# Routing three quarters of the tokens of a mixture-of-experts layer inside the attention loop

## The chip, the cores and the metric

The kernel runs on one core of a Trainium2 chip. The metric is the device time of one execution in microseconds (us), as a median of several runs. The core has five engines that run their own instruction streams: TensorE (PE in the profile, with its weight loads as PEld), VectorE (DVE), ScalarE (ACT), GpSimd (POOL) and SyncE (SP). In this kernel SP issues the plain DMAs and POOL issues the indirect ones (scatters whose row numbers come from a tensor). The engines wait for each other through semaphores.

## What is computed

Three layers follow each other: path signatures projected to 128 features, attention inside sequences of 64 steps with 8 heads, and a feed-forward layer that adds one shared expert and one of 8 routed experts per token:

```python
h = tok(x, W, b)                          # signature, depth 4, then a projection
h = h + attn(layernorm(h), ...)
xf = layernorm(h)                         # 4096 tokens with padding, 128 features
logits = xf @ gate_w.T                    # 8 experts
wts, idx = jax.lax.top_k(logits, 1)       # one expert each
wts = softmax(wts)                        # of one value: 1
hh = silu(xf @ w1[e].T) * (xf @ w3[e].T)  # e = idx of the token
y = hh @ w2[e].T
y = y + gelu(xf @ sw1.T) @ sw2.T          # the shared expert, for all tokens
h = h + y
```

## The kernel before, in words

The 4096 tokens (64 sequences of 64) are 32 tiles of 128 tokens (`TILES`). The work has three stages.

**The loop.** Iteration i of 32 does attention for tile i, the signature features of tile i + 3 and the projection of tile i + 2, and finishes tile i - 1: its second layer norm gives `x2n`, which ACT keeps in `x2[:, t, 0:128]` (L561) and PE transposes. The transposed tile is spilled by SP to `x2_columns` (L368), and PE's `router` makes its 8 logits, which DVE stores (`keep_logits`, L888). Each engine has its own function `iteration`; the middle iterations run in a hardware loop (`Fori(2, TILES - 3)`, `Fori(1, TILES - 3)` on POOL) and the last three are written out. On POOL an iteration is: level 3 of the signature, `root(0, ...)` (the square root of the first norm, L458), the rest of level 3, `root(1, ...)` for tile i - 1, and `add_channels(i + 2)` (L449 to L453), whose sum PE's `accumulate` waits for. SP's queue holds, per iteration, `by_head` (four copies of the value rows, L363, the second half waiting for the attention of the tile before) and `spill` (L368).

**The tail of the loop and the shared expert.** The 32 tiles are 8 groups of 4 (`GROUPS`). `up(g)` makes 12 wide matmuls from the group's columns, ACT applies the gelu, `down(g)` makes 16 matmuls (32 records), and DVE adds the result to `h` (`add_shared`, L1030), which SP then writes to `out` (L398). The first two groups are started within the last iterations. While this runs, the tokens are routed. DVE picks each token's expert as a one-hot matrix `oh` (5 operations on 256 columns, L1043 to L1047), PE multiplies it by a strictly triangular matrix and by ones (ranks within a tile and totals of a tile), DVE turns these into a row number `pos` for each token (L1051 to L1071): tokens of one expert are consecutive, and each expert begins at a multiple of 128. POOL then scatters the 32 tiles of `x2`, one indirect DMA each (L507), into the DRAM tensor `sorted_rows` of 39 x 128 rows; a row is 128 values and the token's number (`ROW` = 129, 516 bytes). 39 tiles (`SORTED`) suffice for any routing. All rows were filled before with zeros and an impossible token number, by three DMAs of 13 tiles each ahead of the loop (L347), from a buffer that lies in `x2`; ACT waits for these before iteration 0 (L635).

**The experts.** For each of the 39 sorted tiles SP loads 128 rows (L404, L409), PE transposes them and multiplies them by the weights of the expert whose number it reads from the table `exp_i`, and POOL adds the result to `out` by an indirect DMA (L515), which drops rows with an impossible number. PE begins this stage when all 8 groups are added (`added`), and SP loads the first rows when group 5 is added and all scatters have landed.

The order is written out by hand: each engine executes its stream in order, so an instruction that waits holds up all that stand behind it on its engine.

Of the kernel before, what the change touches and what calls it, by code (L numbers as in the profile page):

```python
# [39 lines left out]
P = 128  # L40
# [28 lines left out]
FILL = SORTED // 3  # L69
SMALL_STEPS, NORM_STEPS, ROUTE_STEPS = 21, 9, 21  # L70
# [13 lines left out]
def build(nc, x_next, x_prev, w_low, w_high, tok_b, wqkv, u_qkv, wout_t, u_columns, b_out,  # L84
          scalars, gate_t, w13_t, w2_t, sw1_t, sw2_t, square, mask_c, steps, out):
    with ExitStack() as ctx:
# [7 lines left out]
        sorted_rows = nc.dram_tensor("sorted_rows", [SORTED * P, ROW], F32, kind="Internal").ap()  # L94
# [32 lines left out]
        fill, t3, t4, v3 = parts(x2[:].rearrange("p t r -> p (t r)"), FILL * ROW, in_c, in_c, in_c)  # L127
        fill = fill.rearrange("p (t r) -> p t r", r=ROW)
# [14 lines left out]
        stepc = sb("stepc", [P, EXPERTS + TILES + SORTED])  # L143
        rev_expert = stepc[:, 0:EXPERTS]
        tile_edges = stepc[:, EXPERTS:EXPERTS + TILES]
        tile_index = stepc[:, EXPERTS + TILES:]
# [55 lines left out]
        def taker(*hosts):  # L202
# [3 lines left out]
            def take(*shape):  # L206
# [3 lines left out]
                for part in parts:  # L210
# [20 lines left out]
        oh = late(TILES, EXPERTS)  # L231
        pick = late(TILES, EXPERTS)
        best = sb("best", [P, 2, TILES])
        tot = late(EXPERTS, TILES)
        incl = late(EXPERTS, TILES)
        zeros = late(EXPERTS * TILES)
        rt = sb("rt", [P, 8, EXPERTS])
        off = late(EXPERTS, TILES)
        over = late(EXPERTS, TILES)
        pos_f = late(TILES)  # L240
        pos = sb("pos", [P, TILES], U32)
        upt = late(SORTED, EXPERTS)
        exp_f = late(SORTED)
        exp_i = sb("exp_i", [P, SORTED], I32)
# [11 lines left out]
                    for n in range(2))  # L256
# [46 lines left out]
                                                  sem("scattered"))  # L303
        xg_hi, xg_lo, gelu_done = sem("x_group_hi"), sem("x_group_lo"), sem("gelu_done")
# [17 lines left out]
        def _(sp):  # L322
# [50 lines left out]

            by_head(0)
            with sp.Fori(0, 2 * GROUP) as t:
# [5 lines left out]
            with sp.Fori(2 * GROUP, TILES - 2) as t:  # L381
                by_head(t + 1)
                spill(t)
# [8 lines left out]

            for g in range(GROUPS):
# [6 lines left out]
                if g == GROUPS - 3:  # L400

                    sp.wait_ge(scattered, 16 * TILES)
                    for j in range(2):
                        sp.dma_start(rows[:, j, :], sorted_rows[j * P:(j + 1) * P, :]).then_inc(rows_in[j], 16)  # L404
            with sp.Fori(2, SORTED - 2, 2) as j:
                for k in range(2):
                    sp.wait_ge(rT_psum, j + (k - 1))
                    sp.wait_ge(id_kept, j + (k - 1))
                    sp.dma_start(rows[:, k, :], sorted_rows[bass.ds((j + k) * P, P), :]).then_inc(rows_in[k], 16)  # L409
            sp.wait_ge(rT_psum, SORTED - 2)  # L410
            sp.wait_ge(id_kept, SORTED - 2)
            sp.dma_start(rows[:, 0, :], sorted_rows[(SORTED - 1) * P:SORTED * P, :]).then_inc(rows_in[0], 16)
# [3 lines left out]
        def _(pool):  # L416
# [4 lines left out]
            nc.gpsimd.memset(fill[:, :, 0:DIM], 0.0)  # L421
            nc.gpsimd.memset(fill[:, :, DIM:ROW].bitcast(I32), NO_TOKEN).then_inc(filled, 1)
# [37 lines left out]

            def iteration(i, f, u, acc, prev=True):
# [29 lines left out]
            add_channels(1)  # L491
            iteration(0, True, True, True, False)
            with pool.Fori(1, TILES - 3) as i:
                iteration(i, True, True, True)
            iteration(TILES - 3, False, True, True)
# [1069 lines left out]
```

## Time and profile before

| | |
|---|---|
| median of 3 runs | 719.44 us (716.79 to 720.65) |
| the profiled execution: its own time | 718.2 us |
| its span, first to last instruction | 716.2 us |
| mean granted TensorE clock | 0.971 |
| PE busy | 653.1 us, 91% |
| PE weight loads busy | 521.1 us, 73% |
| DVE busy | 414.3 us, 58% |
| ACT busy | 295.8 us, 41% |
| POOL busy | 321.6 us, 45% |
| DMA packets, volume | 40993, 44.79 MB |

The page gives each engine's busy time, the same in 40 equal slices of the span, the DMA queues, the chain of work that ended last, and the costliest groups of instructions with the idle time ahead of them and what ended it. Views of single stretches give the busy times between two points, and the timeline lists the instructions in order. "issue" as a releaser means that the engine waited for nothing that the profile shows. PE multiplies at 2.4 GHz when the granted clock is 1.0 and at 1.2 GHz when it is 0.5. An fp32 matmul is recorded as two.

### The profile page before, as it was taken

How to read it: one execution, taken by the hardware profiler on the slowest of the kernel's cores; microseconds unless marked ns; L12 is line 12 of the kernel's file. 1: busy time of each engine (PE TensorE's matmuls, PEld its weight loads, DVE VectorE, ACT ScalarE, POOL GpSimd, SP SyncE). 2: the span in 40 equal slices, each digit the busy share in tenths (PEclk: the TensorE clock that was granted, in tenths of full speed). 3: DMA queues.
4: the chain of work that ended last, by engine and by line, in shares of the span. 5: the costliest groups of instructions: out<-in, count | busy, mean ns of one | idle time of the engine just before them, and what ended most of it. 6: DMA issues, size and time to landing. Idle time of an engine off the chain costs nothing.

```text
span 716.2 us, 13835 instructions
## 1 busy us (share of the span) xinstructions
PE 653.1 (91%) x3960; PEld 521.1 (73%) x3993; DVE 414.3 (58%) x1087; ACT 295.8 (41%) x701; POOL 321.6 (45%) x336
## 2 busy tenths in 40 slices
PE   5989999999999999999999999988753989999993
PEld 4767878887888778878887888766741867777772
DVE  7876667666766666667666666663710234455451
ACT  4234453445344443544454445437520434334440
POOL 3454455444545454544454445320376005444553
PEclk9999999999999999999999999999975799999998
DMA  8951112212211121112111211122621112322230
GB/s 315 223 197 30 38 33 47 48 37 62 53 42 37 33 59 37 37 33 62 33 37 33 62 33 37 35 62 67 208 83 52 46 48 40 42 40 41 37 41 5
DMA packets 40993, 44.79 MB, mean 63 GB/s; under 512 B 6416, under 2 KB 29712, under 8 KB 40592
## 3 DMA queue, kind: packets, MB, share of 16 engines
q1 hardware_dynamic: 34336, 40.34, 21.5%
q0 software_dynamic: 6640, 4.22, 4.2%
q8 instruction: 10, 0.16, 0.1%
q14 instruction: 7, 0.06, 0.0%
HBM read 16.78 MB, written 11.44 MB: 39 GB/s over the span
## 4 chain that ended last, share of the span: by engine, by line
PE 84%; issue 6%; DVE 5%; POOL 2%; ACT 1%; DMA 0%; SPq 0%; POOLq 0%; DVEq 0%
PE bank L1136 75%; PE bank L1448 3%; PE bank L1192 2%; PE bank L1338 2%; POOL z L449 1%; PE bank L1431 1%; PE bank L1251 1%; PE bank L1242 0%; PE bank L1197 0%; PE bank L1196 0%; POOL z L451 0%; DVE ident_b L960 0%; DVE z L833 0%; POOL out L515 0%; DVE vow L728 0%
## 5 line engine op out<-in xcount | busy, mean ns | idle before, releaser
L1136 PE MATMUL bank<-whigh,uth 128*128 128x512 f32 x512 | 167.6, 408 | 1.4 <-DVE lowt L728 1.4
L1136 PEld LDWEIGHTS bank<-whigh,uth 128*128 128x128 f32 x512 | 91.5, 188 | 27.3 <-issue 7.7
L515 POOL DMA_INDIRECT out<-z,ids x39 | 60.8, 1559 | 94.4 <-ACT z L691 94.1
L1136 PE MATMUL bank<-whigh,utl 128*128 128x512 f32 x256 | 101.0, 395 | 0.0
L458 POOL TENSOR_TENSOR rstd<-rstd,powers 128x1 f32<-128x1 f32 x64 | 35.2, 550 | 141.2 <-DVE rstd L820 83.7
L449 POOL TENSOR_TENSOR z<-z 128x512 f32<-128x512 f32 x32 | 42.2, 1320 | 94.0 <-DVE z L833 94.0
L1136 PE MATMUL bank<-xT,qkw 128*128 128x128 f32 x512 | 62.4, 275 | 0.0
L1109 DVE COPY xvp<-bank 128x512 f32<-128x512 f32 x39 | 27.0, 692 | 59.5 <-PE bank L1448 59.5
L1136 PEld LDWEIGHTS bank<-xT,qkw 128*128 128x128 f32 x512 | 59.7, 192 | 0.1
L833 DVE TENSOR_TENSOR z<-bank,v 128x512 f32<-128x512 f32 x64 | 44.1, 690 | 22.7 <-PE bank L1136 18.3
L1136 PEld LDWEIGHTS bank<-whigh,utl 128*128 128x128 f32 x256 | 48.1, 188 | 11.6
L1136 PE MATMUL bank<-whigh,vow 128*128 x117 | 49.0, 527 | 0.0
L567 ACT ACTIVATE xqk<-bank,fac 128x512 f32<-128x512 f32 x64 | 43.9, 689 | 7.2 <-PE bank L1136 5.9
L585 ACT ACTIVATE prob<-prob 128x512 f32<-128x512 f32 x32 | 20.2, 633 | 62.1 <-DVE prob L909 62.1
L591 ACT COPY pt<-bank 128x512 f32<-128x512 f32 x32 | 18.8, 588 | 64.2 <-PE bank L1338 64.2
L842 DVE TENSOR_TENSOR h<-bank,tokb 128x128 f32<-128x128 f32 x32 | 9.3, 292 | 59.8 <-PE bank L1136 59.8
L1136 PE MATMUL bank<-vow,xTh 128*128 128x512 f32 x128 | 42.8, 416 | 1.1 <-ACT xqk L567 1.1
L680 ACT ACTIVATE z<-bank 128x512 f32<-128x512 f32 x39 | 23.3, 598 | 49.2 <-PE bank L1136 30.2
L444 POOL TENSOR_TENSOR e3l<-e,e3h 128x512 fp32r<-128x512 f32 x31 | 40.4, 1304 | 6.2 <-DVE xn L854 4.9
L1136 PEld LDWEIGHTS bank<-xvp,pt 128*64 128x64 f32 x512 | 30.1, 137 | 17.8 <-issue 17.4
L1136 PE MATMUL bank<-levels,xvp 128*128 x312 | 41.4, 276 | 0.7 <-ACT z L691 0.5
L574 ACT COPY xvo<-bank 128x512 f32<-128x512 f32 x64 | 37.7, 588 | 10.2 <-PE bank L1136 8.8
(204 smaller groups left out, 1437.4 us busy)
## 6 DMA issues: line engine op xcount, KB each, us to landing
xvp<-xvo SPq DMA_DIRECT2D x128, 128.0 KB, 2.3
w<-w_t SPq DMA_DIRECT2D x1, 4096.0 KB, 19.3
sorted_rows<-x SPq DMA_DIRECT2D x3, 838.5 KB, 18.0
prob<-sorted_rows SPq DMA_DIRECT2D x39, 64.5 KB
w<-w_high SPq DMA_DIRECT2D x4, 512.0 KB, 5.9
x_columns<-x2t SPq DMA_DIRECT2D x32, 64.0 KB, 1.6
xg_in<-x_columns SPq DMA_DIRECT2D x8, 256.0 KB
levels<-w_t SPq DMA_DIRECT2D x1, 2048.0 KB, 7.5
```

The costliest lines, as they stand in the source:

```text
L444: G.tensor_tensor(e3l[:], e3[:], e3h[:].bitcast(F32), ALU.subtract).then_inc(e3_lo, 1)
L449: G.tensor_tensor(z4[:], z[:, 0:4, :], z[:, 4:8, :], ALU.add).then_inc(tree, 1)
L458: G.tensor_tensor(rstd[:, n, 1:2], rstd[:, n, 0:1], powers[:, 0:1], ALU.pow) \
L515: nc.gpsimd.indirect_dma_start(out=out[:, :], out_offset=bass.IndirectOffsetOnAxis(ap=ids[:, j:j + 1], axis=0), in_=y[:, j % 2, :], in_off ...
L567: A.activation(xqk[:, :, 4 * n:4 * n + 4, :], B[5 + n][:].rearrange("p (s h k) -> p s h k", s=2, h=4), ACT.Copy, scale=fac[:, 1:2]).then_i ...
L574: A.copy(xvo[:, n, :, :].rearrange("p c d -> p (c d)"), B[7 - 2 * n][:]) \
L585: A.activation(prob[:], prob[:], ACT.Exp).then_inc(exp_done, 1)
L680: nc.scalar.activation(act[:, k, :], B[1 + 2 * k][:], ACT.Silu).then_inc(silu_done, 1)
L833: V.tensor_tensor(z[:, cs, :], B[1 + half][:].rearrange("p (c d) -> p c d", c=4), spread(v[:, bass.ds(s, 1), cs].rearrange("p o c -> p (o ...
L1109: V.tensor_copy(hidT[:, k, :, :].rearrange("p c t -> p (c t)"), B[5][:]).then_inc(hT_sb, 1)
L1136: return T.matmul(out_, lhsT, rhs, start=start, stop=stop)
L1448: last = T.transpose(B[5][:, col(c)], hid[:, k, col(c)], ident)
```

## The change

24 of the 32 tiles (`EARLY`) are routed and scattered while the loop still runs. The rows now go to a region of 4096 rows per expert, so that a tile's rows can be placed before the totals are known: `sorted_rows` grows from 39 to 264 slabs of 128 rows. A table `row_i`, filled on DVE, gives each of the 39 expert tiles the first of its rows, and SP reads it for each load.

- The three fills ahead of the loop become 24 fills of 11 slabs (726 KB each), one per iteration 0 to 23 on SP's queue behind the spill, from a buffer `blank` of one row per partition. ACT's wait for the fills goes; POOL waits for them before the first scatter.
- DVE does the choice of the expert for 24 tiles at the end of iteration 25, the running sums at the end of 26, the row numbers at the end of 27. PE does the two rank matmuls (192 columns) in iteration 26, ACT copies them out of the bank.
- POOL issues the 24 scatters in iterations 28 (3, at its end), 29 (3 after `root(0)`, 2 after `root(1)`, 3 after `add_channels`), 30 (3 after `root(0)`, 6 after `root(1)`) and 31 (4 after `root(1)`); the last 8 follow after the loop.
- The same steps for 8 tiles stay after the loop (64 columns in place of 256), with one more sum for the base; `count`, the tile table and the new row table follow behind the row numbers.
- The hardware loops are cut: PE and ACT have `Fori(2, 26)`, iteration 26 written out, `Fori(27, 29)`; DVE has 25 to 28 written out, POOL 28.

```diff
-FILL = SORTED // 3
+EARLY = 24
+FILL, FILLS = 11, 24
+SLABS = FILL * FILLS
+CHOOSE_AT, RANK_AT, PLACE_AT, SCATTER_AT = EARLY + 1, EARLY + 2, EARLY + 3, EARLY + 4
...
@@ sync
-            sp.wait_ge(filled, 1)
-            for n in range(SORTED // FILL):
-                sp.dma_start(sorted_rows[n * FILL * P:(n + 1) * FILL * P, :].rearrange("(t p) r -> p t r", p=P),
-                             fill).then_inc(fill_sent, 16)
...
+            def fill(t):
+                sp.dma_start(sorted_rows[bass.ds(t * (FILL * P), FILL * P), :].rearrange("(n p) r -> p n r", p=P),
+                             spread(blank[:], 1, [P, FILL, ROW])).then_inc(fill_sent, 16)
...
+            with sp.Fori(2 * GROUP, FILLS) as t:
+                by_head(t + 1)
+                spill(t)
+                fill(t)
...
+            def load_rows(j, k):
+                row = sp.value_load(row_i[0:1, bass.ds(j, 1)], min_val=0, max_val=(SLABS - 1) * P)
+                sp.dma_start(rows[:, k, :], sorted_rows[bass.ds(row, P), :]).then_inc(rows_in[k], 16)
...
@@ gpsimd
+            def scatter(tiles):
+                for t in tiles:
+                    nc.gpsimd.indirect_dma_start(
+                        out=sorted_rows[:, :], out_offset=bass.IndirectOffsetOnAxis(ap=pos[:, t:t + 1], axis=0),
+                        in_=x2[:, t, :], in_offset=None).then_inc(scattered, 16)
...
                 if f:
                     level3_rest(i + 3)
+                if is_tile(i, SCATTER_AT + 1):
+                    scatter(range(3, 6))
+                if is_tile(i, SCATTER_AT + 2):
+                    scatter(range(11, 14))
                 if prev:
                     root(1, ln2, i - 1)
+                if is_tile(i, SCATTER_AT + 1):
+                    scatter(range(6, 8))
+                if is_tile(i, SCATTER_AT + 2):
+                    scatter(range(14, 20))
+                if is_tile(i, SCATTER_AT + 3):
+                    scatter(range(20, EARLY))
                 if u:
                     add_channels(i + 2)
+                if is_tile(i, SCATTER_AT):
+                    pool.wait_ge(pos_ready, 1)
+                    pool.wait_ge(x2_kept, EARLY)
+                    pool.wait_ge(ids_written, 1)
+                    pool.wait_ge(fill_sent, 16 * FILLS)
+                    scatter(range(3))
+                if is_tile(i, SCATTER_AT + 1):
+                    scatter(range(8, 11))
...
@@ scalar
+                if is_tile(i, RANK_AT):
+                    a.wait_ge(rank_psum, 1)
+                    A.copy(ranks_early.rearrange("p n m -> p (n m)"), B[6][:, 0:2 * EARLY * EXPERTS]) \
+                        .then_inc(rank_kept, 1)
...
@@ vector
+            def running(ts, counts, tot_, incl_, part):
+                n = ts.stop - ts.start
+                start, count, base = (rt[:, 3 * part + m, :] for m in range(3))
+                rstep(V.tensor_copy(tot_, counts.rearrange("p t e -> p e t")))
+                rstep(V.tensor_tensor_scan(incl_.rearrange("p e t -> p (e t)"), tot_.rearrange("p e t -> p (e t)"),
+                                           zeros[:, 0:n * EXPERTS], 0.0, ALU.add, ALU.add))
+                V.memset(start[:, 0:1], 0.0)
+                rstep(V.tensor_copy(start[:, 1:EXPERTS], incl_[:, 0:EXPERTS - 1, n - 1]))
+                V.tensor_tensor(count, incl_[:, :, n - 1], start, ALU.subtract)
+                rstep(V.tensor_tensor(base, slab_start, start, ALU.subtract))
+                rstep(V.tensor_tensor(incl_, incl_, tot_, ALU.subtract))
+                if part:
+                    rstep(V.tensor_tensor(base, base, rt[:, 1, :], ALU.add))
+
+            def place(ts, ranks, oh_, pick_, tot_, incl_, pos_, part):
+                n = ts.stop - ts.start
+                rstep(V.tensor_tensor(incl_, incl_, spread(rt[:, 3 * part + 2, :], 2, [P, EXPERTS, n]), ALU.add))
+                rstep(V.tensor_tensor(pick_, incl_.rearrange("p e t -> p t e"), ranks, ALU.add))
+                rstep(V.tensor_tensor(pick_, pick_, oh_, ALU.mult))
+                rstep(V.reduce_sum(pos_, pick_, axis=AX))
+                V.tensor_copy(pos[:, ts], pos_).then_inc(pos_ready, 1)
...
+            choose(slice(EARLY, TILES), oh, pick)
+            d.wait_ge(rank_psum, 2)
+            running(slice(EARLY, TILES), te_bank[1], tot, incl, 1)
+            place(slice(EARLY, TILES), te_bank[0], oh, pick, tot, incl, pos_f, 1)
...
@@ tensor
+                if is_tile(i, RANK_AT):
+                    pe.wait_ge(route, CHOOSE_STEPS)
+                    n = EARLY * EXPERTS
+                    mm(B[6][:, 0:n], below, oh_early[:].rearrange("p t e -> p (t e)"))
+                    mm(B[6][:, n:2 * n], ones, oh_early[:].rearrange("p t e -> p (t e)")).then_inc(rank_psum, 1)
...
-            with pe.Fori(2, TILES - 3) as i:
+            with pe.Fori(2, RANK_AT) as i:
+                iteration(i, True, True, True)
+            iteration(RANK_AT, True, True, True)
+            with pe.Fori(RANK_AT + 1, TILES - 3) as i:
```

## Rows read from the trace of the kernel before

**Rows 1.** The page, part 2: 40 slices of 17.9 us; digits are tenths.
```profile
PE   5989999999999999999999999988753989999993
PEclk9999999999999999999999999999975799999998
```
**Rows 2.** Stretches: length, busy us (x instructions) of PE, PEld, DVE, ACT, POOL; clock, DMA.
```profile
512.30:524.20 11.90, 11.42 (x76) 10.33 (x77) 5.87 (x12) 4.12 (x8) 9.22 (x9) 1.00 0.46 133
524.20:556.50 32.30, 10.58 (x28) 6.05 (x26) 1.90 (x4) 3.93 (x7) 22.54 (x23) 0.56 0.21 65
```
**Rows 3.** Timeline inside the second stretch: start, length, engine, operation [idle before].
```profile
541.08 0.29 PEld L1136 LDWEIGHTS bank<-vow,sw 128*128 128x128 f32 x1 [1.12 <-issue]
541.77 0.59 PE L1136 MATMUL bank<-vow,sw 128*128 128x512 f32 x1 [0.82 <-issue]
```
**Rows 4.** The tile pos: the scatters; durations in ns, then first and last start in us.
```profile
L507 POOL DMA_INDIRECT sorted_rows<-x,pos x32: 954/959/1363, 512.3 to 552.6; - x32
```
**Rows 5.** DMA queues from 520 to 556: packets, MB, share of 16 engines.
```profile
q0 software_dynamic: 866, 1.79, 15.3%
q1 hardware_dynamic: 672, 0.52, 4.9%
```
**Rows 6.** Timeline of the shared-FFN groups, before and after the slow stretch.
```profile
512.78 3.07 PE L1136 MATMUL bank<-vow,sw 128*128 128x512 f32 x12 [3.02 <-DVE vow L728]
...
563.33 0.48 PE L1136 MATMUL bank<-uth,sw 128*128 128x512 f32 x1
...
569.71 3.05 PE L1136 MATMUL bank<-vow,sw 128*128 128x512 f32 x12
...
576.16 0.61 PE L1136 MATMUL bank<-sw,xqk 128*128 128x128 f32 x4
...
579.94 0.69 DVE L1030 TENSOR_TENSOR h<-h,bank 128x512 f32<-128x512 f32 x1 [2.88 <-PE bank L1136]
```
**Rows 7.** Timeline of the routing chain after the loop, on DVE and PE.
```profile
502.56 0.42 DVE L1044 TENSOR_TENSOR e<-logits,best 128x256 f32<-128x256 f32 x1
...
505.16 1.03 PE L1136 MATMUL bank<-levels,sq 128*128 128x256 f32 x4
...
506.75 0.69 DVE L1052 TENSOR_TENSOR_SCAN g<-e,g 128x256 f32<-128x256 f32 x1
...
507.68 0.17 DVE L1058 TENSOR_TENSOR rt<-g,rt 128x8 f32<-128x8 f32 x1
```
**Rows 8.** Timeline of DVE between two trips of the loop.
```profile
462.22 0.29 DVE L842 TENSOR_TENSOR h<-bank,tokb 128x128 f32<-128x128 f32 x1 [1.89 <-PE bank L1136]
```
**Rows 9.** Timeline of POOL, iterations 29 to 31.
```profile
471.65 1.27 POOL L449 TENSOR_TENSOR z<-z 128x512 f32<-128x512 f32 x1 [2.36 <-DVE z L833]
...
476.69 0.55 POOL L458 TENSOR_TENSOR rstd<-rstd,powers 128x1 f32<-128x1 f32 x1 [1.88 <-DVE rstd L850]
481.68 0.55 POOL L458 TENSOR_TENSOR rstd<-rstd,powers 128x1 f32<-128x1 f32 x1 [4.44 <-DVE rstd L820]
...
499.13 0.55 POOL L458 TENSOR_TENSOR rstd<-rstd,powers 128x1 f32<-128x1 f32 x1 [3.98 <-DVE rstd L820]
```
**Rows 10.** The fills: issue times (ns), landing; then SP's queue from 24 to 28.
```profile
L347 SPq DMA_DIRECT2D sorted_rows<-x x3: 433/4568/5203, 11.9 to 17.6; - x3
DMA to landing us min/median/max: 13.1/18.0/18.7
q1 hardware_dynamic: 1451, 0.74, 124.9%
```
**Rows 11.** Timeline of SP's queue in the loop.
```profile
80.25 2.39 SPq L363 DMA_DIRECT2D xvp<-xvo  x4
87.85 0.34 SPq L368 DMA_DIRECT2D x_columns<-x2t  x1
94.48 2.39 SPq L363 DMA_DIRECT2D xvp<-xvo  x4
```
**Rows 12.** Waits on SP's queue in the expert stage: us in total, times, longest.
```profile
SPq L408 <- DVE ids L1097: 83.8, 34, 4.4
```

More of the change, by code:

```diff
@@ L380, in _ @@
             load_group(1)
-            with sp.Fori(2 * GROUP, TILES - 2) as t:
+            with sp.Fori(2 * GROUP, FILLS) as t:
+                by_head(t + 1)
+                spill(t)
+                fill(t)
+            with sp.Fori(FILLS, TILES - 2) as t:
                 by_head(t + 1)
@@ L400, in _ @@
                 if g == GROUPS - 3:
+                    sp.wait_ge(pos_ready, 4)
                     sp.wait_ge(scattered, 16 * TILES)
                     for j in range(2):
[L404 removed]
+                        load_rows(j, j)
             with sp.Fori(2, SORTED - 2, 2) as j:
@@ L491, in _ @@
             add_channels(1)
+            nc.gpsimd.iota(x2[:, :, DIM:ROW].bitcast(I32), pattern=[[P, TILES], [1, 1]], base=0,
+                           channel_multiplier=1).then_inc(ids_written, 1)
             iteration(0, True, True, True, False)
-            with pool.Fori(1, TILES - 3) as i:
+            with pool.Fori(1, SCATTER_AT) as i:
                 iteration(i, True, True, True)
+            iteration(SCATTER_AT, True, True, True)
             iteration(TILES - 3, False, True, True)
@@ L498, in _ @@
             root(1, ln2, TILES - 1)
-            nc.gpsimd.iota(x2[:, :, DIM:ROW].bitcast(I32), pattern=[[P, TILES], [1, 1]], base=0,
-                           channel_multiplier=1).then_inc(ids_written, 1)
-            pool.wait_ge(pos_ready, 1)
+            pool.wait_ge(pos_ready, 2)
             pool.wait_ge(x2_kept, TILES)
-            pool.wait_ge(ids_written, 1)
-            for t in range(TILES):
-                nc.gpsimd.indirect_dma_start(
-                    out=sorted_rows[:, :], out_offset=bass.IndirectOffsetOnAxis(ap=pos[:, t:t + 1], axis=0),
-                    in_=x2[:, t, :], in_offset=None).then_inc(scattered, 16)
+            scatter(range(EARLY, TILES))
             for g in range(GROUPS):
@@ L639, in _ @@
             iteration(1, True, True, True, False)
-            with a.Fori(2, TILES - 3) as i:
+            with a.Fori(2, RANK_AT) as i:
+                iteration(i, True, True)
+            iteration(RANK_AT, True, True)
+            with a.Fori(RANK_AT + 1, TILES - 3) as i:
                 iteration(i, True, True)
@@ L892, in x_group_lo, with rstep, choose @@
                 remainder(xgl[k], xg_in[:, k, :], xgh[k], xg_lo)
+            n_route = 0
+            def rstep(ins):
+                nonlocal n_route
+                ins.then_inc(route, 1)
+                n_route += 1
+                d.wait_ge(route, n_route)
+            def choose(ts, oh_, pick_):
+                te = [P, ts.stop - ts.start, EXPERTS]
+                top, first = best[:, 0, ts], best[:, 1, ts]
+                rstep(V.tensor_reduce(top, logits[:, ts, :], AX, ALU.max))
+                rstep(V.tensor_tensor(pick_, logits[:, ts, :], spread(top, 2, te), ALU.is_equal))
+                rstep(V.tensor_tensor(pick_, pick_, spread(rev_expert, 1, te), ALU.mult))
+                rstep(V.tensor_reduce(first, pick_, AX, ALU.max))
+                rstep(V.tensor_tensor(oh_, spread(rev_expert, 1, te), spread(first, 2, te), ALU.is_equal))
+            def running(ts, counts, tot_, incl_, part):
[18 more added lines that the diff above has]
+                V.tensor_copy(pos[:, ts], pos_).then_inc(pos_ready, 1)
             def iteration(i, f, u, acc, prev=True, older=True):
@@ L935, in iteration @@
                     features_lo(i + 3)
+                te_early = ranks_early.rearrange("p n (t e) -> p n t e", e=EXPERTS)
+                if is_tile(i, CHOOSE_AT):
+                    d.wait_ge(lg_sb, EARLY)
+                    choose(slice(0, EARLY), oh_early[:], pick_early)
+                if is_tile(i, RANK_AT):
+                    d.wait_ge(rank_kept, 1)
+                    running(slice(0, EARLY), te_early[:, 1], tot_early, incl_early, 0)
+                if is_tile(i, PLACE_AT):
+                    place(slice(0, EARLY), te_early[:, 0], oh_early[:], pick_early, tot_early, incl_early,
+                          pos_early, 0)
             n_norm = 0
@@ L1012, in _ @@
             iteration(1, True, True, True, True, False)
-            with d.Fori(2, TILES - 3) as i:
+            with d.Fori(2, CHOOSE_AT) as i:
+                iteration(i, True, True, True)
+            for i in range(CHOOSE_AT, TILES - 3):
                 iteration(i, True, True, True)
```

114 lines of the change are left out of this document (51 added, 63 removed).

## The prediction, made before the changed kernel ran

> **What bounds the kernel now.** I read the slices first. PE is nearly full in all of them except for two places: the start, and the slices around three quarters of the span, where it falls to 3 tenths while its granted clock falls too [rows 1]. Cut into stretches, the second place has a sharp edge. From 512.3 to 524.2 PE is busy 11.4 of 11.9 us; in the next 32.3 us only 10.6, with 28 matmuls, and at a mean clock of 0.56, close to the lower level of 1.2 GHz [rows 2]. That is the shared expert, whose work is all available. The timeline says what kind of idleness it is: single weight loads and matmuls, 0.70 us apart, each released by "issue", so no semaphore of this kernel and no operand is being waited for [rows 3]. DVE, ACT and SP only wait for PE there. What else runs is POOL: the 32 scatters, from 512.3 to 552.6, of 0.96 us with some 0.3 us between them, as 31 starts take 40.3 us [rows 4]. The last ends at 553.6, and PE is back to speed some 4 us later. The DMA engines aren't full: the scatters' queue takes 15% of them, the other 5% [rows 5]. So what holds PE isn't bandwidth. Scatters side by side with slow PE issue is a coincidence in time, with one oddity: for the first 12 us of scattering PE wasn't slowed.
>
> **What the slow stretch costs.** After it, PE needs 6.38 us per pair of an up and a down (563.33 to 569.71), and the last down takes some 3.75 us (576.16 to 579.9) [rows 6]. From 512.78 there are 5 pairs and one down left: 5 x 6.38 + 3.75 = 35.65 us, which would end at 548.4. It ends at 579.9. The stretch costs 31.5 us, the slow clock included. The experts can't start earlier, since they wait for the last group; behind it they need what they need now (136 us of the span).
>
> **The routing chain after the loop.** DVE's operations on 256 columns take 0.42 us, the scan 0.69, those on 8 columns 0.17 [rows 7]; some 20 of them hold `x_group_lo(3)` back, and PE waits 3.0 us for it at 512.8 [rows 6]. PE's own rank matmuls take 1.03 us [rows 7]. With 64 columns PE's part falls to a quarter, 0.26 us (-0.77). DVE's chain behind the ranks, 11 short operations at about 0.2 us, is an estimate of 2.4 us from these rows; it then ends inside `down(1)` (3.7 us) and the 3.0 us wait goes. Gain together 3.8 us, if the loop costs nothing.
>
> **What the loop pays, by engine.** PE: 192 columns in iteration 26, 1.03 x 0.75 = 0.8 us, all on its path. ACT: one copy out of the bank between the exponential and `x_hi`; ACT idles there, free. DVE: 5 operations of 192 columns (0.35 us and a hop of 0.04: 2.0 us) at the end of iteration 25, 1.8 us in 26, 1.8 us in 27. The next thing DVE does is `keep_logits` and then a wait of 1.9 us for PE's `accumulate` [rows 8]; that wait is the cover. What sticks out is 0.1 us in each, 0.3 us in all; with no cover it would be 5.6 us.
>
> POOL: each scatter is taken at 1.26 us, the first 1.66 [rows 4]. I laid them into POOL's timeline [rows 9], where what counts is the instruction behind each burst. In iteration 28 three scatters end at 464.5, `root(0)` for tile 30 is late by 1.0 us, and DVE has slack for that. In 29: the first three and two delay `add_channels(31)` by 0.35 us (due at 471.65), which PE's `accumulate` passes on: +0.35. The three behind it run to 478.95, but `root(0)` of tile 31 is due at 476.69: 2.3 us late, of which DVE absorbs 1.1: +1.2 us through the softmax to PE's transposes. In 30 the three before `root(1)` (due at 481.68) add 0.4, since PE waits for x2n there; the six behind it end at 491.5 and meet no one before 494. In 31 the four delay the last `root(1)` (499.13) by 1.1. Together 3.0 us. Loop in all: 0.8 + 0.3 + 3.0 = 4.1, less rounding 3.8 to 4.1. That takes back the 3.8 us of the routing chain. The bounds of the scatter's duration are its rows' ends, 0.95 and 1.36 us [rows 4]; at the upper end the bursts are a third longer and cost 3 us more. A gain is excluded there, as nothing that follows a burst gets earlier.
>
> Here the Trainium skill speaks against the change. SBUF — State Buffer, section "Who interferes with whom", says that GpSimd, which writes the descriptors of its DMAs, is locked out while VectorE runs an operation in a two-port mode. Taken fully, 24 scatters that each wait for a DVE operation would be longer by that. The rows bear it out little: with DVE half busy most scatters still took 0.96 us. The sum goes by the rows.
>
> **The fills.** Three fills of 838 KB go from before the loop. Nothing waited for them: ACT's wait ended long before its first iteration. In their place are 24 of 726 KB. While fills had the queue alone it moved 0.74 MB in 4 us with all engines full [rows 10], so a fill occupies them for about 4 us. It goes out behind the spill (87.9 in the trip shown) and the next copies behind it are issued at 94.5 [rows 11], 6.6 us later: the fill has drained by then. If not, these copies land later; ACT's next overwrite of the buffer gives them some 4.6 us beyond their landing time. Issuing took 0.43 us with the ring free and up to 5.2 us with it full [rows 10]; both end within the 6.6 us. Cost taken: 0. Bounds: 0 to 1 us in each of 24 if they don't drain. SP's table read for each row load is unseen so far; PE's reads of such a table show as 0.24 us of "issue", and SP idles 2.5 us per tile in the expert stage [rows 12]. Free. The tables on DVE come behind the row numbers and have 35 us until they are read.
>
> **The last 8 scatters** run from about 511.5 for 10.2 us and land some 3 us later: before PE slowed in the old kernel (12 us in). I take them as free; by the old price of a slow stretch (31.5 us lost in 32.3) the worst is 10 us.
>
> **Sum.** Loop +3.8, routing chain -3.8, slow stretch -31.5: span 716.2 - 31.5 = 684.7, own time 718.2 - 31.5 = 686.7. The median is 1.2 us above the profiled time: 687.9. Own range of this case, from the bounds: 683 to 694. Forecast: 688.
>
> **Rivals.**
> (a) A part of the slow stretch stays. PE issue suffers under every burst that lasts, whether in iteration 30 (9 scatters almost in a row, some 11 us) or after the loop (8 scatters, 10 us). For: PE slowed only after 12 us, so length matters, and near-continuous scattering from 461 to 491 is longer than that. Against: the gaps of up to 3 us, in which POOL adds channels. Losing 7 to 26 of the 31.5 us: 695 to 714, middle 703.
> (b) The slow stretch moves into the loop as a whole. This is the one that ends slower. The place is iterations 28 to 31, where PE has four times the instructions per us left to issue. If PE slows from the first scatter on, 24 scatters (30.6 us) and 8 (10.2) lose 5/6 of their time: 34 us, and POOL's 3.8 us are no longer hidden; with the clock at its lower level behind each, 720 to 728, 725 in the middle. It decides at the point where the 12 us of grace don't renew in a gap. The old stretch of 32 us did 5 us of work; that is where the 5/6 come from [rows 2].
> (c) The slowness has nothing to do with scatters, but with where PE's instructions lie: it began in the middle of a written-out loop body, 12 us behind the start of the scatters. Then it stays or turns up elsewhere: 716 to 723. Against: it ended with the scatters, although the body was then only a quarter through, and the queues show no packet of an instruction queue in the stretch [rows 5]. The Trainium skill, Runtime: NRT & Kernel Launch, section "Instruction fetch mechanics", says that the engines' instructions are streamed in blocks and that a branch out of the loaded blocks stalls; no row here shows a fetch in flight while PE crawls.
> (d) The fills don't drain between spill and copies. If one took the 18 us that fills took from issue to landing at the start, behind the loads [rows 10], instead of 4, each trip of 14.2 us (80.25 to 94.48) would stretch to 18 [rows 11]: 24 x 4 = 96 us slower, some 810.
>
> **Chances.** Forecast 0.62, better than its range 0.02; (a) 0.19; (c) 0.05; (b) 0.09, of which 0.02 within the 0.5%; (d) 0.03. Within 0.5% (716 to 723, about what a measurement of this kernel can tell from no change): 0.07. Slower by more: 0.10. Faster by more: 0.83. Range: 683 to 714, which holds the forecast and (a), 0.81.
>
> **What would show it.** Right: between the last iteration and the experts PE has no row with 0.7 us steps of "issue", the shared-expert groups follow at 6.4 us, the clock stays 1.0; iterations 0 to 24 keep their 14.2 us; from the end of iteration 27 to the first `up` after the loop PE loses 3 us, at `root(0)` of tile 31. (a): single-file PE rows beside the bursts of 6 or 8. (b): the same in 29 to 31. (c): the same with no scatter near. (d): trips longer than 14.2 us with ACT's copy waiting for a DMA. It would be wrong if the slow issue needs only a scatter, not a row of them, or if the loop's POOL order costs more than the instruction behind each burst.

## The result and the profile after

| | before | after |
|---|---|---|
| median | 719.43 us (716.79 to 720.65, 4 runs) | 692.41 us (691.7 to 695.3, 4 runs) |
| profiled execution: own time, span | 718.2, 716.2 us | 691.94, 690.1 us |
| mean granted clock | 0.971 | 0.985 |
| PE busy | 653.1 us, 91% | 647.0 us, 94% |
| DMA packets, volume | 40993, 44.79 MB | 70133, 59.70 MB |

The ratio of the times is 0.964 (95% interval 0.962 to 0.966). The forecast was 688; the measured time is 4.4 us above that and inside the forecast's own range of 683 to 694.

The page of after, part 2, in slices of 17.3 us. The hole of [rows 1] is gone, in PE and in its clock:

```profile
PE   5999999999999999999999999999789989999993
PEclk9999999999999999999999999999999999999997
```

What is left in its place are two shallower slices, from 483 to 518 us. POOL's scatters, by the tile `pos` (durations in ns, first and last start in us), now lie mostly ahead of that place, where [rows 4] had all of them in one row from 512.3 to 552.6:

```profile
L485 POOL DMA_INDIRECT sorted_rows<-x,pos x32: 956/962/1303, 464.4 to 526.8; - x32
```

To see where the rest went I used SP's spill of each tile as a mark, since it appears once per iteration in both kernels. First after, then before:

```profile
399.80 0.34 SPq L372 DMA_DIRECT2D x_columns<-x2t  x1
...
461.27 0.34 SPq L372 DMA_DIRECT2D x_columns<-x2t  x1
...
507.98 0.34 SPq L372 DMA_DIRECT2D x_columns<-x2t  x1
```
```profile
400.84 0.34 SPq L368 DMA_DIRECT2D x_columns<-x2t  x1
...
457.75 0.34 SPq L368 DMA_DIRECT2D x_columns<-x2t  x1
...
500.85 0.34 SPq L368 DMA_DIRECT2D x_columns<-x2t  x1
```

At 400 us after is 1.0 us ahead, at the end of the loop 7.1 us behind. With the shared-expert groups behind it, the account is (in us; the measured parts are rounded one by one):

| part of the span | predicted | measured |
|---|---|---|
| start, to the spill at 72 us | 0 | -1.5 |
| iterations with a fill | 0 | +0.5 |
| iterations 25 to 28 (ranks, DVE's steps) | +1.1 | +4.6 |
| iterations 29 to 31 (POOL's bursts) | +3.0 | +3.6 |
| last spill to `up(3)` | -3.8 | -2.2 |
| `up(3)` to the last group | -31.5 | -31.1 |
| experts | 0 | +0.1 |
| span | -31.5 (its terms add up to -31.2) | -26.1 |

Two parts of the loop, one after another. PE in iteration 27: the scores wait 1.42 us for `keep_logits`, and DVE's timeline shows what stands ahead of that copy.

```profile
435.94 1.08 PE L1217 MATMUL bank<-xqk,xT 128*64 128x512 f32 x4 [1.42 <-DVE logits L938]
```
```profile
432.49 0.57 DVE L966 COPY tail<-tail 128x192 f32<-128x192 f32 x1
433.09 1.32 DVE L967 TENSOR_TENSOR_SCAN tail<-tail,zeros 128x192 f32<-128x192 f32 x1
...
434.93 0.36 DVE L973 TENSOR_TENSOR tail<-tail 128x192 f32<-128x192 f32 x1
435.32 0.17 DVE L938 COPY logits<-bank 128x8 f32<-128x8 f32 x1
```

The scan of 192 columns takes 1.32 us, where the one of 256 columns in [rows 7] took 0.69. POOL in iteration 30, part of its timeline (start, length, [idle before]):

```profile
481.73 0.96 POOL L485 DMA_INDIRECT sorted_rows<-x,pos  x1 [0.30 <-issue]
482.72 0.57 POOL L479 TENSOR_TENSOR rstd<-rstd,powers 128x1 f32<-128x1 f32 x1
483.48 1.10 POOL L485 DMA_INDIRECT sorted_rows<-x,pos  x1 [0.19 <-issue]
...
486.36 0.96 POOL L485 DMA_INDIRECT sorted_rows<-x,pos  x1 [0.30 <-issue]
487.35 0.57 POOL L479 TENSOR_TENSOR rstd<-rstd,powers 128x1 f32<-128x1 f32 x1
```

Neither root has an idle time before it: each starts as the burst ahead of it ends, while before it had waited 1.9 and 4.4 us for DVE [rows 9]. PE passes that on: 2.4 of the 3.6 us are in this iteration. There it waits 1.27 us for POOL's `add_channels` where it had waited 0.49, 1.20 instead of 0.59 ahead of the transposes of `prob`, and 2.42 instead of 1.57 for `x2n`. Behind the loop, PE's stretches (length, then busy us of PE, PEld, DVE, ACT, POOL; clock, DMA share, GB/s):

```profile
509.00:514.00 5.00, 4.66 (x17) 3.81 (x18) 1.31 (x6) 2.56 (x5) 0.00 (x0) 0.68 0.94 352
517.70:530.90 13.20, 13.06 (x90) 11.81 (x89) 8.82 (x21) 6.42 (x13) 7.92 (x8) 1.00 0.43 124
530.90:555.50 24.60, 23.25 (x168) 21.27 (x166) 7.49 (x15) 10.66 (x23) 0.00 (x0) 1.00 0.24 69
```

The first holds `up(2)`: at a mean clock of 0.68 it takes 4.2 us instead of 2.9. In the other two PE is full, beside the last 8 scatters and after them. `up(3)` starts without a wait, where [rows 6] had 3.0 us:

```profile
517.70 3.05 PE L1217 MATMUL bank<-vow,sw 128*128 128x512 f32 x12
```

One more thing stands beside the scatters, in before and in after. DVE's add of a group waits only for the last matmul of that group's `down`. In before one of these adds starts at 558.16, 25.1 us after that matmul has ended (533.02) and 22.7 us after PE has begun on the next group (535.46). The one ahead of it waits 4.81 us although PE is still at full speed then; in after one waits 4.11 us beside the last 8 scatters:

```profile
523.51 0.69 DVE L1030 TENSOR_TENSOR h<-h,bank 128x512 f32 x1 [4.81 <-remote]
558.16 0.69 DVE L1030 TENSOR_TENSOR h<-h,bank 128x512 f32 x1 [24.38 <-remote]
```
```profile
529.11 0.69 DVE L1133 TENSOR_TENSOR h<-h,bank 128x512 f32 x1 [4.11 <-remote]
```

"remote" means that the profile shows no instruction whose end released the wait. ACT has such waits too (6.55 us in before, 5.30 in after). So the scatters go together with late starts on three engines, not on PE alone.

### The profile page after: what moved, and what is told of

It is laid out like the page before. It is cut to its first block, busy times and chain, and to the rows that moved or that the text cites. A ratio compares the mean times of both kernels' runs of the same rounds, so it can differ in the third digit from the quotient of the medians.

```text
span 690.1 us, 13988 instructions
## 1 busy us (share of the span) xinstructions
PE 647.0 (94%) x3964; PEld 519.6 (75%) x3997; DVE 420.6 (61%) x1110; ACT 295.9 (43%) x702; POOL 322.1 (47%) x336
## 2 busy tenths in 40 slices
DMA packets 70133, 59.70 MB, mean 87 GB/s; under 512 B 6752, under 2 KB 58848, under 8 KB 69728
## 4 chain that ended last, share of the span: by engine, by line
PE 83%; DVE 6%; issue 4%; POOL 4%; DMA 1%; ACT 0%; SPq 0%; ACTq 0%; DVEq 0%; POOLq 0%
PE bank L1217 74%; PE bank L1539 3%; PE bank L1273 2%; PE bank L1426 2%; POOL sorted_rows L485 1%; POOL z L470 1%; PE bank L1522 1%; PE bank L1332 1%; PE bank L1323 0%; PE bank L1278 0%; POOL z L472 0%; PE bank L1277 0%; POOL out L558 0%; DVE utl L777 0%; DVE z L883 0%
## 5 line engine op out<-in xcount | busy, mean ns | idle before, releaser
L558 POOL DMA_INDIRECT out<-prob,ids x39 | 60.9, 1561 | 94.0 <-ACT prob L740 92.5
L1217 PE MATMUL bank<-xT,qkw 128*128 128x128 f32 x512 | 63.9, 279 | 0.0
L1217 PEld LDWEIGHTS bank<-xT,qkw 128*128 128x128 f32 x512 | 61.3, 196 | 0.1
L1217 PE MATMUL bank<-xqk,xT 128*64 128x512 f32 x128 | 34.5, 618 | 8.4 <-DVE logits L938 4.2
## 6 DMA issues: line engine op xcount, KB each, us to landing
sorted_rows<-blank SPq DMA_DIRECT2D x24, 709.5 KB, 5.7
```

What stands on the lines that cost most here:

```text
L558: nc.gpsimd.indirect_dma_start(out=out[:, :], out_offset=bass.IndirectOffsetOnAxis(ap=ids[:, j:j + 1], axis=0), in_=y[:, j % 2, :], in_off ...
L1217: return T.matmul(out_, lhsT, rhs, start=start, stop=stop)
```

## The experiments

The theory was that a long unbroken row of scatters makes PE issue slowly, and that a break lets it recover. The rivals were the place of PE's instructions, and that any scatter does it. Kernels named b are the kernel before with an edit, those named a the changed kernel with one. Where only one time is given it is a single run; each stands beside the kernel before on the same chip. The first four ran on one chip, with before at 719.24 us.

**1. Only 8 of the 32 scatters.**

```diff
-                    sp.wait_ge(scattered, 16 * TILES)
+                    sp.wait_ge(scattered, 16 * 8)
...
-            for t in range(TILES):
+            for t in range(8):
                 nc.gpsimd.indirect_dma_start(
```

> The kernel before with 24 of its 32 scatters left out (tiles 8 to 31 are not scattered, so their routed part is missing) and the rows loaded after 8 landings. Theory 1, long scattering next to PE makes its issue crawl, from about 12 us in: no crawl at all, the shared-expert groups follow at 6.4 us, and the span falls by the 31.5 us of the slow stretch to 685. Theory 2, the crawl belongs to the place of PE's instructions (a page, a loop body): the stretch from 524 to 556 stays and the span stays at 714 to 718.

The routed part of 24 tiles is missing from what this kernel computes. Measured 685.59 us, span 683.8. The stretch that was slow is full, at full clock:

```profile
524.20:549.00 24.80, 24.80 (x186) 23.17 (x185) 8.10 (x13) 11.81 (x22) 0.00 (x0) 1.00 0.25 70
```

The span is 32.4 us shorter than in the trace of before, but not all of that is the stretch: 0.3 comes from the start and 2.2 from the expert stage, whose rows differ here (134.1 us instead of 136.3). From `up(3)` to the last group's add it is 37.3 us instead of 67.2, so 29.9; `up(3)` itself took 4.4 us instead of 2.9 at a granted clock of 0.5 to 0.74, and without that the stretch would be worth 31.4, against the 31.5 of the sum. PE's work isn't held up by 8 scatters in a row. DVE's add beside them is: it waits 4.95 us for "remote" and starts at 523.87, some 3 us after PE's `down` has ended (520.6), which here costs no time. The scatters are the cause of the stretch; which property of them is not said yet.

**2. PE's loop over the groups written out.** All 32 scatters stay.

```diff
-            with pe.Fori(2, GROUPS - 3, 2) as g:
+            for g in range(2, GROUPS - 3, 2):
```

> The kernel before with PE's hardware loop over the groups 2 to 5 of the shared expert written out; nothing else. Theory 2 (the crawl hangs on the loop body or on where its instructions lie): the slow stretch vanishes or moves, the span falls to about 685 or changes by several us. Theory 1 (the scatters): the crawl starts again some 12 us into the scattering and ends with it, the span stays at 714 to 719.

Measured 716.6 us, span 714.6. The slow stretch is where it was, with PE's instructions in another place:

```profile
524.20:556.50 32.30, 11.36 (x29) 6.38 (x28) 1.32 (x3) 3.93 (x7) 21.45 (x22) 0.59 0.21 64
```

That, and experiment 4, in which PE's code is that of after, speaks against rival (c).

**3. The 32 scatters with two breaks.**

```diff
             for t in range(TILES):
+                if t == 8:
+                    pool.wait_ge(added, 4)
+                if t == 16:
+                    pool.wait_ge(added, 6)
```

> The kernel before with its 32 scatters in runs of 8, 8 and 16: POOL waits for 4 added groups before the ninth and for 6 before the seventeenth. Theory 1 with a grace of some 12 us that renews in a pause: no crawl in the first two runs (512 to 523, 530 to 540), the groups end near 548 to 550, the third run begins near 542 and the experts begin when it has landed, near 567: span about 703. Theory 1 without renewal (the count of scatters matters): PE crawls from about 530 on. Theory 2: the crawl begins at 524 whatever POOL does.

Measured 705.27 us, span 703.2. POOL's breaks were 5.6 and 2.4 us:

```profile
522.84 0.96 POOL L511 DMA_INDIRECT sorted_rows<-x,pos  x1 [0.30 <-issue]
529.41 1.16 POOL L511 DMA_INDIRECT sorted_rows<-x,pos  x1 [5.62 <-DVE h L1034]
...
542.18 0.96 POOL L511 DMA_INDIRECT sorted_rows<-x,pos  x1 [2.36 <-DVE h L1034]
```

and PE stayed full through the whole of it, 23 scatters long:

```profile
513.40:550.00 36.60, 35.88 (x252) 32.83 (x252) 13.48 (x23) 15.51 (x29) 22.52 (x23) 1.00 0.34 104
```

In before PE slowed at about the tenth. So it is the row without a break that matters, and what PE is spared at first comes back after a break of 2.4 us (one run). What the 16 of the last row do to PE beyond the seventh isn't seen, since its work on the groups ends at 549.9. The 19.7 us over experiment 1 are another cost: from there PE waits until the last scatters have landed.

```profile
565.78 0.83 PE L1435 MATMUL bank<-sq,prob 128*128 128x128 f32 x2 [15.88 <-DVE h L1034]
```

Two things come at nearly the same time there. SP loads the first rows from `sorted_rows` at 563.42, and the add of the last group, for which PE waits as well, starts only at 564.99, 15 us after PE's last matmul of the groups:

```profile
564.99 0.69 DVE L1034 TENSOR_TENSOR h<-h,bank 128x512 f32<-128x512 f32 x1 [16.41 <-remote]
```

So DVE's add started late beside the scatters at a time when PE had nothing left to do.

**4. The changed kernel with all scatters behind the loop.**

```diff
-                if is_tile(i, SCATTER_AT + 1):
-                    scatter(range(3, 6))
...
-            scatter(range(EARLY, TILES))
+            scatter(range(TILES))
```

> The changed kernel with all its 32 scatters after the loop, in one run; the early routing, the fills and the tables stay. Theory 1: the crawl comes back from about 12 us behind the first scatter (which now starts near 514) to its end near 555, and the time goes back to 712 to 720; the 3.6 us that POOL's bursts cost in the loop are saved, so the loop ends at about 504 in place of 508. Theory 2: the time stays near 690 or below, since PE's instructions haven't moved.

Measured 722.72 us, span 720.9: 3.5 us above the kernel before. The routing in the loop and the fills alone bring nothing, and the slow stretch is back:

```profile
526.00:560.00 34.00, 8.24 (x25) 5.54 (x25) 2.58 (x4) 3.93 (x7) 22.31 (x24) 0.56 0.21 62
```

The spills price both costs of the loop apart. Up to iteration 28 they are late as in after:

```profile
400.39 0.34 SPq L372 DMA_DIRECT2D x_columns<-x2t  x1
...
461.90 0.34 SPq L372 DMA_DIRECT2D x_columns<-x2t  x1
...
504.91 0.34 SPq L372 DMA_DIRECT2D x_columns<-x2t  x1
```

61.51 us to the fourth spill against 56.91 in before, +4.6; then 43.01 against 43.10, nothing. In after the latter stretch takes 46.71: POOL's bursts cost 3.6 to 3.7 us, and DVE's steps and the ranks the other 4.6.

**5 and 6. The two costs moved.** The slip of iterations 25 to 28 has two possible causes: DVE's steps standing ahead of `keep_logits`, or the cut loops. In the first kernel each step goes behind `keep_logits` of the next iteration; in the second, the bursts are also cut so that fewer scatters stand ahead of `root` (2 go behind the loop).

```diff
                 if prev and older:
                     keep_logits(i - 2)
+                if is_tile(i, CHOOSE_AT + 1):
+                    d.wait_ge(lg_sb, EARLY)
+                    choose(slice(0, EARLY), oh_early[:], pick_early)
...
-                if is_tile(i, CHOOSE_AT):
-                    d.wait_ge(lg_sb, EARLY)
-                    choose(slice(0, EARLY), oh_early[:], pick_early)
```
```diff
-                    scatter(range(11, 14))
+                    scatter(range(7, 10))
...
-                    scatter(range(14, 20))
+                    scatter(range(10, 19))
...
+            scatter(range(22, EARLY))
             pool.wait_ge(pos_ready, 2)
```

> The changed kernel with DVE's three early routing steps moved from the end of iterations 25, 26 and 27 to the place right behind keep_logits in iterations 26, 27 and 28; nothing else. Theory P (PE's scores wait for keep_logits, which the steps hold back, so the cover there was next to nothing): the 3.8 us that the spills of iterations 25 to 28 slipped go to under 1 us, since the 1.9 us wait for accumulate now covers the steps and PE's transposes have slack: 689 us. Theory Q (DVE is simply full there, or POOL and DVE slow each other): the slip stays at 3 to 4 us, 692 us.

> As the run before, and the 24 early scatters laid into POOL's own gaps: 2 behind the sums of iteration 28, 3 + 1 + 1 in iteration 29, 3 + 9 in iteration 30, 3 in iteration 31, 2 + 8 after the loop. Theory P (a burst costs what it makes the instruction behind it late): root(0) of tile 31 comes on time, the 3.6 us of the bursts fall to under 1, and PE doesn't lose its clock before up(2): another 3 to 4 us, 685 us. Theory R (the scatters themselves slow PE in the loop): the 3.6 us stay, 689 us. The nine in a row last 11.4 us, just under the 11 to 13 us after which PE crawled: should it crawl there, 687 to 692.

These ran on another chip, where the kernel before took only 696.89 us (694.78 to 697.93, 7 runs); on this, more below. The first took 689.26 us (688.23 to 689.34), ratio to before 0.989 (0.987 to 0.991), the second 684.48 us (684.14 to 684.86), 0.983 (0.980 to 0.985). The trips of the loop take 14.2 us in the traces of both chips, so the loop can be compared across them. In the first, PE's scores no longer wait, though the scan is as long as it was.

```profile
432.27 0.17 DVE L938 COPY logits<-bank 128x8 f32<-128x8 f32 x1
432.46 0.37 DVE L966 COPY tail<-tail 128x192 f32<-128x192 f32 x1
432.87 1.32 DVE L967 TENSOR_TENSOR_SCAN tail<-tail,zeros 128x192 f32<-128x192 f32 x1
```
```profile
434.44 1.08 PE L1217 MATMUL bank<-xqk,xT 128*64 128x512 f32 x4
```

Its spills come at 400.71 and 458.44, 57.73 us, +0.8, about the 0.92 us that the rank matmuls take. The place of the steps ahead of `keep_logits` was the cause, 3.7 us, and not the cut loops. In the second kernel the four spills behind that come 0.8 us later than in before instead of 3.6: at 457.33 and 501.27, 43.94 us against 43.10. Its `up(2)` is still slow, mean clock 0.66 from 502.5 to 507, so the gaps that the bursts leave in iterations 29 to 31 aren't the cause; that part of the expectation failed. Experiment 4 says the same: no scatter stands in its loop, PE works 3.94 us in the 6 us ahead of `up(2)` as in before (3.95), and `up(2)` ran at 0.60. Nor is it only the changed kernel: `up(2)` was slow in all six traces of changed kernels, and in three of the eight with the old loop (experiments 3, 7 and 8, at 0.59). What these 1.3 us hang on stays open.

**7 and 8. Smaller breaks.** Does a break that POOL makes without idling help: waiting for landing after every 8 scatters, or one short operation, into a spare tile, after every 3?

```diff
             for t in range(TILES):
+                if t and t % 8 == 0:
+                    pool.wait_ge(scattered, 16 * t)
```
```diff
             for t in range(TILES):
+                if t and t % 3 == 0:
+                    G.tensor_tensor(spare[:, t:t + 1], powers[:, 1:2], powers[:, 0:1], ALU.pow)
```

> The kernel before with POOL waiting, before each eighth scatter, until all scatters so far have landed. If a pause of some 3 us with nothing in flight renews the grace: no crawl, the groups end at 548 to 550, the scatters end near 562 (40 us and three pauses of 3 us), the experts start when they have landed, near 566: 703 us. If a pause must be longer, or the number of scatters counts: crawl from about 528 on, 716 to 722.

> The kernel before with one small POOL computation (128 x 1, 0.55 us) ahead of every third scatter; no wait is added. In the changed kernel PE didn't crawl beside 12 scatters that only such operations broke up. If an operation between the scatters is what spares PE: no crawl, groups end near 549, scatters near 559, experts from 563: 699 to 703 us. If only time without scatters does: crawl from about 525 until the last scatter, some 6 us longer than before: 720 to 726 us.

Measured 702.82 and 703.34 us, neither with a slow stretch. It would be wrong to count that for either: the unchanged kernel beside them took 696.89 us, 22 us less than in the comparisons so far. They say nothing of the slow stretch, only what the end of the scatters costs where PE isn't slowed: a last scatter 5.0 and 6.4 us later than in [rows 4], for some 6 us of time.

**9 and 10. Both kernels again**, to know whether the slow stretch belongs to the kernel or to a chip.

> The kernel before, unchanged, for a trace on whatever chip this call gets. In the call before this one it ran at 696.9 us on its chip, 22.5 us under the 719.4 us of the table, although all 32 scatters stood in one row. If long scattering makes PE crawl on every chip (theory 1 as I had it), that number must come from elsewhere, and this trace shows the crawl from 524 to 556 and 716 to 719 us. If the crawl belongs to the chip as well (theory 1 with a condition): either 716 to 719 us with the crawl, or 695 to 698 us with the groups ending near 549, PE idle until the last scatter has landed near 556.7, and the experts from about 560.

> The changed kernel, unchanged, beside the kernel before on the same chip. Where the kernel before crawls: a ratio of about 0.964 as first measured. Where it doesn't: the change still takes away PE's wait for the last scatters (some 8 to 11 us between the end of the groups at 549 and the experts) and gives back 5 us by its later arrival at the groups, so 690 to 693 us against 697: a ratio of 0.990 to 0.995.

On another chip than those of experiments 1 to 8, before took 718.78 us (718.11 to 720.12, 7 runs) and its traced run 720.17; after took 694.02 (693.69 to 695.04), ratio 0.966 (0.964 to 0.967). The trace of before has the slow stretch again:

```profile
524.20:556.50 32.30, 6.72 (x27) 4.94 (x26) 2.59 (x4) 3.93 (x7) 21.88 (x23) 0.60 0.22 65
```

**11 and 12.** Experiment 8 and the second kernel of 6 again.

> The kernel before with a small POOL computation ahead of every third scatter, again, because the first time its neighbour, the unchanged kernel, ran at 696.9 us and so without the slow stretch. If the kernel before stands at 716 to 720 us here: an operation between scatters spares PE if this gives 700 to 704 us, and doesn't if it gives 720 to 726. If the kernel before stands at 697 again, this says nothing on the crawl and gives 703.

> The rearranged version of the changed kernel (DVE's steps behind keep_logits, scatters in POOL's gaps), again, to stand beside a kernel before that crawls. It took 684.5 us where the kernel before took 696.9. With 9 scatters in a row in the loop and 2 + 8 behind it, no run reaches 12 us: 684 to 687 us also where the kernel before crawls and takes 719, a ratio near 0.953. If nine in a row are already too many there: 690 us or more.

Another chip again, and one more on which before is quick: 696.45 us (695.62 to 698.43, 7 runs). The operations between scatters took 702.06, so that question stays open. The rearranged kernel took 685.46 us (684.37 to 686.48), ratio 0.983 (0.981 to 0.986), 11 us ahead of before even there.

## Why the prediction was right, and by how much it was off

**The slow stretch** was priced at 31.5 us. The groups from `up(3)` on took 36.1 us against the 35.65 worked out, and experiment 1 gives 31.4 once what doesn't belong to the stretch is taken off. The mechanism behind the price, that the row of scatters holds PE back, was only a coincidence in time when I predicted; experiments 1, 3 and 4 show it: without the long row no slow stretch, with it in the changed kernel the stretch again. Where PE was seen to slow, it did so 10.7 to 13.5 us after the first scatter, so behind 9 to 11 of them. The 8 behind the loop came near that limit: one hiccup of 0.4 us, 11.4 us behind the first. "Free" was right for them, with little to spare. One reading was wrong: that DVE and ACT only wait for PE in the stretch. The add at 558.16 had its input some 25 us earlier, so the price was right while the picture of it, slow issue on PE alone, was too narrow.

**POOL's bursts**, 3.0 us predicted by laying scatters into the timeline, cost 3.6 (3.7 by experiment 4). Most of it arises, as worked out, up to `x2n` in iteration 30, but the parts differ: 0.8 us at `add_channels(31)`, 0.6 at `root(0)` and 0.85 at `root(1)`, where 0.35, 1.2 and 0.4 were taken. That the sum came so near is in part luck. The rule of the Trainium skill that I weighed there (SBUF — State Buffer, "Who interferes with whom": GpSimd locked out in VectorE's two-port modes) isn't borne out to any size: the median scatter took 0.962 us with 24 of the 32 beside the loop's DVE work, the longest 1.30.

**DVE's cover** is the step that failed. The sum took 0.3 us for the steps at the end of iterations 25, 26 and 27, since DVE then waits 1.9 us for `accumulate` [rows 8]. But `keep_logits` stands between them and that wait, and PE's scores need it much earlier. The rows of before did show that copy; I read the first idle time behind the steps as cover for all that stands in between, which holds only for what nobody else waits for. Durations were also taken too low: the steps took 2.7, 2.8 and 2.9 us where 2.0, 1.8 and 1.8 stood, most of all the scan with 1.32 us. Measured 3.7 us where 0.3 stood; experiment 5 gives it back by a move of the steps alone.

**The routing chain** behind the loop brought 2.2 us instead of 3.8. The wait of 3.0 us went as predicted. PE's rank matmuls brought 0.5 instead of 0.77 (0.39 us from their start to the next matmul, 0.86 before), and `up(2)` at a mean clock of 0.68 takes 1.3 back. No term stood for the clock.

**The fills** were taken as free: a trip takes 14.25 us against 14.23, in all 0.5 us. SP's timeline in a trip shows the fill at 86.92, and its median landing time on the page is 5.7 us, less than the 6.1 us to the next copies:

```profile
86.38 0.34 SPq L372 DMA_DIRECT2D x_columns<-x2t  x1
86.92 0.40 SPq L380 DMA_DIRECT2D sorted_rows<-blank  x1
93.00 2.39 SPq L367 DMA_DIRECT2D xvp<-xvo  x4
```

By the landing time that is a margin of 0.4 us, where I had one of 2.6. **The row table** on SP and the experts are as predicted. **The start** looks 1.5 us quicker, but I don't credit the change with it: the kernels with the old start reach the spill shown first above anywhere from 399.2 to 400.8 us in their traces, those with the new one from 399.6 to 400.9.

**The sum and its range.** The terms give 31.2 us, not 31.5: 4.1 us of the loop were set at 3.8 to cancel the routing chain, with no row for it. The range of 683 to 694 is narrower than the bounds named beside it, 3 us for longer scatters, up to 24 for the fills and 10 for the last 8, so it was a judgement and not their sum. That the result fell inside it says less than the account by parts.

**The rivals.** (b) and (c) are refuted for this change: PE doesn't crawl in the loop, as the roots and `add_channels` break up the row (12 scatters from 479.2 to 495.5 with two roots between them had no slow PE). (a) is refuted but for the hiccup, and (d) by the trips; its price was also too high, since 24 trips at 4 us more on 688 are 784 and not 810. With (c) falls the instruction fetch of which the Trainium skill tells (Runtime: NRT & Kernel Launch, "Instruction fetch mechanics"): PE's code without that loop crawled all the same, and no packet of an instruction queue fell in the stretch [rows 5].

## What stays open

What in a row of scatters holds PE back isn't known: the queues had room [rows 5], and nothing in the traces shows a resource that both want. Nor is it known whether the time, the number, or the scatters not yet landed count. The late starts of DVE are the best lead. They are in every trace from the chips where before took about 719 us, in after too, and in none from the two others: beside 8 scatters in a row the add waited 4.95 us for "remote" in experiment 1, and 0.87 us for PE in experiment 7:

```profile
520.06 0.69 DVE L1032 TENSOR_TENSOR h<-h,bank 128x512 f32 x1 [0.87 <-PE bank L1138]
```

Whether a signal from PE comes late or the waiting engine starts late can't be read from the traces. Whether a short POOL operation is break enough wasn't settled either, as both tries fell on chips without the effect; the 12 scatters with two roots between them in after's loop speak for it. And it hangs on the chip: in three comparisons before took 719.4, 719.2 and 718.8 us, in two, on two other chips, 696.9 and 696.5. It wasn't traced on the latter. An estimate: there PE would be done with the groups near 549 as in experiment 7 and wait for the last scatters; shifting the time of experiment 7, 702.8 us with its last scatter at 557.6, by the 5.0 us to the 552.6 of [rows 4] gives 697.8, near the 696.9 measured. The changed kernel wasn't timed on those chips. Its gain there is smaller: experiment 5 lacks 3.7 us of its costs and took 689.3, so some 693 us against 696.9 (an estimate).

## What to carry to other kernels

When an engine idles with nothing to wait for while another one issues a row of indirect DMAs, as here beside 32 in a row, break the row with work the kernel has anyway, or spread it; and test on more than one chip, since the same kernel differed by 22 us. When steps are put ahead of a wait, the wait covers only those instructions between which nobody else waits for: here a copy of 0.17 us stood in between, and cost ten times what the steps were reckoned at. Of a burst on an in-order engine, ask for the instruction right behind it; that gave 3.0 of the 3.6 us. And when an engine slows, look at what its results release: here the add that came 25 us late said more than PE's own lines.

## What the runs showed of the hardware

PE's issue fell to one instruction per 0.70 us or a multiple of that (experiment 4, PE's timeline from 10.6 us behind its first scatter), with the clock following only later (1.00 up to 530 us, 0.53 from 530 to 532):

```profile
525.01 0.79 PE L1204 MATMUL bank<-sw,xqk 128*128 128x128 f32 x2
526.15 0.49 PE L1204 MATMUL bank<-sw,xqk 128*128 128x128 f32 x2 [0.35 <-issue]
...
531.13 0.37 PE L1204 MATMUL bank<-sw,xqk 128*128 128x128 f32 x1 [0.93 <-issue]
532.56 0.37 PE L1204 MATMUL bank<-sw,xvp 128*128 128x128 f32 x1 [1.06 <-issue]
```

A break of 2.4 us in the row of scatters was enough to avoid it, and on two of the chips the kernel before was 22 us quicker, as it would be without it. In all traces from the other chips DVE's adds waited for 4.1 to 24.4 us beside the scatters, even beside 8 in a row, with "remote" as releaser. A DVE scan of 192 columns took 1.32 us beside a working POOL and one of 256 columns 0.69 us beside an idle one. A fill of 709.5 KB (of 1024 bytes; the 726 KB of the change) in rows of 516 bytes landed in 5.7 us (median), took 0.4 us of issue on SP's queue, and lengthened a trip by 0.02 us.
